# Attention scores taken three head pairs at a time, with one and two steps of context in turn, and 13 row sums a group on TensorE

## What is computed

```python
q = _layernorm_scale_only(q, q_ln_scale)
k = _layernorm_scale_only(k, k_ln_scale)
...
scores = jnp.einsum('bshd,bthd->bhst', q / jnp.sqrt(jnp.float32(HEAD_DIM)), k)
causal = jnp.triu(jnp.ones((S, S), dtype=bool), 1)
scores = jnp.where(causal, NEG_INF, scores)
attn = jax.nn.softmax(scores, axis=-1)
ctx = jnp.einsum('bhst,bthd->bshd', attn, v)
```

## Time and profile before

| | before |
|---|---|
| median of three runs | 2451.99 us (2450.62 to 2453.79) |
| the profiled execution's own time | 2452.69 us |
| its span | 2450.9 us |
| share of the span TensorE is busy | 96% |
| VectorE, ScalarE, GpSimd | 73%, 54%, 11% |
| mean granted TensorE clock | 0.979 |

### The profile page before, as it was taken

The page is one execution under the profiler, slowest core; times in us unless marked ns, Lnnn a source line. Parts: engine busy times, 40 slices in busy tenths (PEclk is TensorE's granted clock), DMA queues, the critical chain, the costliest instruction groups (busy, mean ns, idle before and its releaser), DMA issues. The chain is left out here.

```text
span 2450.9 us, 34384 instructions
## 1 busy us (share of the span) xinstructions
PE 2353.8 (96%) x12546; PEld 1404.8 (57%) x12546; DVE 1787.0 (73%) x1821; ACT 1317.0 (54%) x1631; POOL 266.3 (11%) x266
## 2 busy tenths in 40 slices
PE   8999966999999999999999999959999999999997
PEld 7777742333343333443334433338888888888885
DVE  7666664898988989889898898954555565565654
ACT  4444435888888888888888888811111111111111
POOL 1111111210122001221012110100000000000000
PEclk9999977999999999999999999979999999999999
DMA  7766677010550106401064010072021121110100
GB/s 246 244 222 241 215 217 143 23 32 5 107 115 23 32 5 114 108 23 32 6 117 105 23 32 5 5 265 78 18 69 35 36 64 32 44 50 21 35 18 17
DMA packets 126399, 197.36 MB, mean 81 GB/s; under 512 B 14992, under 2 KB 39568, under 8 KB 126224
## 3 DMA queue, kind: packets, MB, share of 16 engines
q1 hardware_dynamic: 126224, 195.10, 28.5%
HBM read 122.70 MB, written 72.35 MB: 80 GB/s over the span
## 5 line engine op out<-in xcount | busy, mean ns | idle before, releaser
L883 ACT ACTIVATE probs<-score 128x1024 f32<-128x1024 f32 (+3 forms) x1152 | 1025.2, 956 | 212.2 <-PE score L801 188.2
L949 DVE TENSOR_TENSOR total<-total,probs 128x2048 f32<-128x2048 f32 (+3 forms) x472 | 983.2, 2083 | 78.5 <-POOL probs L762 35.7
L801 PE MATMUL score<-qstk,kstk 98*128 98x512 f32 (+3 forms) x2304 | 659.4, 408 | 35.4 <-DMA qstk<-shift 18.6
L801 PEld LDWEIGHTS score<-qstk,kstk 98*128 98x128 f32 x2304 | 378.9, 190 | 527.3 <-ACT probs L883 411.1
L817 PE MATMUL ctx_acc<-probs,values 128*32 128x512 f32 (+3 forms) x4608 | 576.7, 573 | 8.3 <-POOL probs L762 8.3
L1288 ACT ACTIVATE hidden<-slot,gate_scale_sb 128x512 f32<-128x512 f32 x128 | 88.3, 690 | 624.9 <-PE slot L1217 624.9
L762 POOL TENSOR_SCALAR_AFFINE_SELECT probs<-probs 128x512 f32<-128x512 f32 x128 | 188.1, 1470 | 1037.2 <-ACT probs L883 1037.2
L1373 DVE SCALAR_TENSOR_TENSOR hidden<-slot,up_scale_sb,hidden 128x512 f32<-128x512 f32 x128 | 96.0, 750 | 262.4 <-ACT hidden L1288 257.7
L817 PEld LDWEIGHTS ctx_acc<-probs,values 128*32 128x32 f32 x4608 | 92.0, 108 | 202.4 <-issue 163.0
L1217 PE MATMUL slot<-xt_hi,wg_sb 128*128 128x512 f32 x512 | 201.8, 394 | 5.2 <-issue 5.2
L1228 PE MATMUL y<-wd_sb,h_hi 128*128 128x512 f32 x512 | 199.4, 389 | 1.4 <-DVE h_lo L1381 1.4
(11 more groups left out here) (101 smaller groups left out, 1984.4 us busy)
## 6 DMA issues: line engine op xcount, KB each, us to landing
qstk<-q_hi SPq DMA_DIRECT2D x64, 256.0 KB
kstk<-k_hi SPq DMA_DIRECT2D x64, 256.0 KB, 9.4
wq_int<-in_wq SPq DMA_DIRECT2D x48, 256.0 KB, 3.0
wq_float<-wq_f SPq DMA_DIRECT2D x48, 256.0 KB, 2.7
x_raw<-in_x_t SPq DMA_DIRECT2D x32, 256.0 KB, 3.6
v_rows<-v_out SPq DMA_DIRECT2D x32, 256.0 KB, 2.1
q_hi<-part_hi SPq DMA_DIRECT2D x32, 256.0 KB, 2.1
q_lo<-part_lo SPq DMA_DIRECT2D x32, 256.0 KB, 2.5
```

The lines of the kernel that those rows point to most:

```text
L801: ins = pe.matmul(score[u % RING][:, i, cut(t):], kstk[0:ROWS, h, kb * P:(kb + 1) * P], qstk[0:ROWS, q_buffer[ch], h, cut(t):], start=True ...
L883: act.activation(probs[:, t % PB, 2 * p:2 * p + 2, cut(t):], score[u % RING][:, :, cut(t):], ACT.Exp).then_inc(exped, 1)
L949: dve.tensor_tensor(into, into, now, ALU.add).then_inc(added, 1)
```

## The change

`scores` now takes one unit instead of one step. TensorE's order becomes 96 runs a group. Run k takes the scores of the units 3k to 3k + 2 (six matmuls). After an odd k comes the context of the one step 3(k - 1)/2, after an even k the context of the two steps 3k/2 - 2 and 3k/2 - 1. Steps whose number is a multiple of three stand alone, all others in pairs. The rule of `by_pe` becomes: every ninth step of the group, where it is not diagonal and not the first or second of its chunk. That gives the 13 steps 9, 27, 36, 45, 54, 63, 72, 81, 99, 108, 117, 126 and 135. All are multiples of three. Before, the ten were places 10, 20 and 30 of their chunks. The programs of ScalarE, GpSimd, VectorE and SyncE stay, apart from what follows from the new list of sums.

```diff
@@ by_pe
-        return not diagonal(t) and t - first[ch] >= ST * 2 and (t - first[ch]) % 10 == 0
+        return not diagonal(t) and t - first[ch] > 1 and t % 9 == 0
@@ scores
-            def scores(g, t):
+            def scores(g, u):
+
+                t, p = divmod(u, 2)
                 ch, kb = steps[t]
-                if t in first:
+                if p == 0 and t in first:
                     mine = q_chunks[q_buffer[ch]]
                     pe.wait_ge(q_in[q_buffer[ch]], 64 * len(mine) * g + 64 * (mine.index(ch) + 1))
-                if kb == ST * ch:
+                if p == 0 and kb == ST * ch:
                     pe.wait_ge(ones_ready, 1 + ch + 1)
                     pe.wait_ge(k_in[ch], 48 * g + 48)
-                for p in range(2):
-                    u = 2 * t + p
-
-                    pe.wait_ge(exped, 2 * NS * g + u + 1)
-                    for i in range(2):
-                        h = 2 * p + i
...
+                pe.wait_ge(exped, 2 * NS * g + u + 1)
+                for i in range(2):
+                    h = 2 * p + i
...
+            def score_phase(g, k, after):
+
+                for u in range(RING * k, RING * k + RING):
+                    if u < 2 * NS:
+                        scores(g, u)
+                    elif after:
+                        scores(g + 1, u - 2 * NS)
+
+            def weigh_phase(g, k):
+
+                for t in ((3 * k // 2 - 2, 3 * k // 2 - 1) if k % 2 == 0 else (3 * (k // 2),)):
+                    weigh(g, t)
+                    if t - 2 in last:
+                        sum_total(g, last.index(t - 2))
+
             def group(g, after):

-                for t in range(NS):
-                    if t + LAG < NS:
-                        scores(g, t + LAG)
-                    elif after:
-                        scores(g + 1, t + LAG - NS)
-                    weigh(g, t)
-                    if t + LAG - T_LAG in last:
-                        sum_total(g, last.index(t + LAG - T_LAG))
+                for k in range(1, 2 * NS // RING + 1):
+                    score_phase(g, k, after)
+                    weigh_phase(g, k)
                 sum_total(g, NCH - 1)

-            for t in range(LAG):
-                scores(0, t)
+            score_phase(0, 0, False)
```

More of the change, by code:

```diff
@@ L549, in by_pe @@
         ch, kb = steps[t]
-        return not diagonal(t) and t - first[ch] >= ST * 2 and (t - first[ch]) % 10 == 0
+        return not diagonal(t) and t - first[ch] > 1 and t % 9 == 0
     adds = [t for t in range(NS) if not by_pe(t)]
     NA = len(adds)
-    assert NS % PB == 0 and 2 * NS % RING == 0
+    assert NS % PB == 0 and 2 * NS % RING == 0 and NS % 3 == 0
     NM = sum(diagonal(t) for t in range(NS))
@@ L785, in _ @@
             pe.sem_inc(totaled, 2)
-            def scores(g, t):
+            def scores(g, u):
+                t, p = divmod(u, 2)
                 ch, kb = steps[t]
-                if t in first:
+                if p == 0 and t in first:
                     mine = q_chunks[q_buffer[ch]]
                     pe.wait_ge(q_in[q_buffer[ch]], 64 * len(mine) * g + 64 * (mine.index(ch) + 1))
-                if kb == ST * ch:
+                if p == 0 and kb == ST * ch:
                     pe.wait_ge(ones_ready, 1 + ch + 1)
                     pe.wait_ge(k_in[ch], 48 * g + 48)
-                for p in range(2):
-                    u = 2 * t + p
-                    pe.wait_ge(exped, 2 * NS * g + u + 1)
-                    for i in range(2):
-                        h = 2 * p + i
-                        ins = pe.matmul(score[u % RING][:, i, cut(t):], kstk[0:ROWS, h, kb * P:(kb + 1) * P],
-                                        qstk[0:ROWS, q_buffer[ch], h, cut(t):], start=True, stop=True)
-                    ins.then_inc(scored, 1)
+                u = 2 * t + p
+                pe.wait_ge(exped, 2 * NS * g + u + 1)
+                for i in range(2):
+                    h = 2 * p + i
+                    ins = pe.matmul(score[u % RING][:, i, cut(t):], kstk[0:ROWS, h, kb * P:(kb + 1) * P],
+                                    qstk[0:ROWS, q_buffer[ch], h, cut(t):], start=True, stop=True)
+                ins.then_inc(scored, 1)
             def weigh(g, t):
```

## The result

The changed kernel takes 2463.33 us, the median of five runs (2461.84 to 2466.55), beside 2451.99 before: a ratio of 1.0049 (95% interval 1.0034 to 1.0064). It is slower, by 11 us where the prediction has 8, and within its range. The profiled execution has a span of 2463.6 us, 12.7 more than before.

What follows compares the result with a forecast made beforehand. The prediction took TensorE, busy in 96% of the span, as the bound. Waits 18.3 - 2.1, round trips -16.3 and sums +2.6 gave +2.5 us a group, +8.0 in all with the first group's 0.5: 2460 us, range 2446 to 2474.

Steps and rivals of the forecast that it cites:

- Round trips: TensorE's switches between scores and context: 144 become 96, 0.34 us each, -16.3 us a group.
- Sums: Strip matmuls of sums on TensorE: 13 in place of 10, 0.86 us each, +2.6 us a group.
- Ordinary ring waits: Score loads awaiting a buffer after 17 full-width single steps without a sum: 0.26 us each, 4.4 a group.
- Short contexts: After last diagonals of 128 columns (steps 18, 30, 66, 90) the next run comes sooner and waits: 3.6 us a group.
- Evacuations: After chunk ends at steps 3, 39 and 111 the evacuation holds ScalarE and TensorE waits: 3.6 us a group.
- The 11 among diagonals: The other single steps without a sum, standing among diagonals: 0.2 us of wait each, 2.2 a group.
- Masks: TensorE waits for masks of steps 2, 8, 44 and 116: 0.65 us each, 2.6 a group.
- The group's end: TensorE's total sum waits for VectorE's late last add: 1.9 us a group, between 0 and 2.5.
- Before's own waits: Mask waits already in the kernel before, subtracted from the new waits: 2.1 us a group.
- The first group: Early changes hidden behind the wait for a q transfer at its step 12: it keeps +0.5 us.
- no change: Rival: restarted loads cost 0.16 us and masks mostly find VectorE's add over; about 2452 us, chance 0.25.
- Faster: Rival: the ring gives more slack, or masks and last add come in time; 2442 us, down to 2398, chance 0.15.

Runs made afterwards that it cites:

- bare pair: bare_before and bare_order, the old and new orders with half of the exponentials and of VectorE's adds left out: 2437.24 and 2380.16 us.
- sums_only: The kernel before, in its old order, with the thirteen new sums in place of its ten: 2466.68 us, ratio to before 1.0062.
- bare_before: The kernel before with half of each exponential and half of each VectorE add left out: 2437.24 us, ratio 0.9948.
- take_sooner: The changed kernel with VectorE taking a chunk's old sums two steps sooner, ahead of the next chunk's place 3 add: 2454.12 us, ratio to before 1.0013.
- sums_moved: The changed kernel with the sums of steps 27 and 63 moved to steps 33 and 69: 2452.53 us, ratio to before 1.0007.
- bare_order: The new order with the ten old sums and half of each exponential and of each VectorE add left out: 2380.16 us, ratio 0.9712.
- half-exponential pair: half_exp_before and half_exp_order, the old and new orders, both with ten sums and half of each exponential left out: 2440.09 and 2416.86 us.
- half_exp_before: The kernel before with each exponential over one head of its pair instead of two: 2440.09 us, ratio 0.9948.
- ten_single: The new order with ten sums, all on single steps, none at place 3 of a chunk: 2438.59 us, ratio to before 0.9944.
- order_only: The new order with the old ten sums at their old places: 2444.89 us, ratio to before 0.9976.
- seven_late: The new order with seven sums and VectorE taking the old sums two steps sooner: 2443.53 us, ratio to before 0.9961.
- half_exp_order: The new order with the ten old sums and each exponential over one head of its pair: 2416.86 us, ratio 0.9854.

## Why the prediction was right, and where it was off

The time is in the range and the way is the one forecast: slower by 11 us, forecast 8. The terms that the prediction named are all there. But that it came out slower rests on a wait that the prediction didn't name, and in that it was lucky: its own terms, at their measured sizes, sum to nothing. By its steps, for a middle group:

- *Round trips, -16.3.* Right. 0.34 in the timelines, 14.3 us a group in the bare pair.
- *Sums, +2.6.* Right for the matmuls. No run shows the three adds off VectorE alone. In sums_only the group grew by more than the matmuls, so they brought nothing that shows there.
- *Ordinary ring waits, 17 x 0.26 = 4.4.* They are there, 17 of them, at 0.17: 2.9. The restart costs what was said. At step 48 the third exponential ends 3.65 behind the start of the run and not 3.71, and the next run starts at 2.61 and not 2.58, so that 0.09 of the 0.26 went.
- *Short contexts, 3.6.* Measured 3.2. *Evacuations, 3.6.* Measured 3.6 (1.0, 1.0 and 1.5). *The 11 among diagonals, 2.2.* Measured 1.8.
- *Masks, 2.6.* Measured 3.0, 0.67 each and 0.96 at step 2. The middle between the bounds was a choice that came out.
- *The group's end, 1.9.* Measured 1.9.
- *Before's own waits, 2.1.* They are 3.4: the rows show only what the matmul side recorded as idle. bare_before has groups 3.3 to 3.5 us shorter than before's, which says the same.
- **Missed: the sum at place 3** of a chunk that opens the bank, 3.3 us a group. The prediction named `sum_total`'s waits and never asked what a sum in the middle of a chunk waits for. The line stands in `weigh` (`if opens:` with `sums_taken`). Before, the first sum came at place 10, behind VectorE's turn at place 4, and its wait never showed. take_sooner and sums_moved each take back 9 to 11 us with it.
- **Missed: the clock**, 1.7 us where it falls, once in each of the two full middle groups of the profiled execution.
- *The first group, +0.5.* Counted to its step 143 it is 3.3 us shorter than before (687.0 against 690.2). Its end wait (1.9) lies behind that mark, so the forecast is -1.4 up to there. 1.7 of the 3.3 are there by step 11, behind the wait for the q transfer, which is 16.6 us in this trace and 18.6 before. The prediction costs the queues at nothing; sums_only, with the old order, has 21.4, so that this may be scatter. The groups differ by -3.3, +4.8, +4.4 and +3.6, and +3.1 behind the last step 143: together the 12.7 us of the two spans.

The named waits are 1.9 us smaller in sum (16.4 for 18.3) and those of before 1.3 larger, which hid 3.2 of the 5.0 missed. With measured sizes the same sum gives 21.4 - 3.4 - 16.3 + 2.6 = +4.3 us for this group, and the trace has +4.4 (308.9 against 304.5). The step of the prediction that failed is the price of the sums, "3 x 0.86", which took them for matmuls alone: at their new places they cost another 3.3 us a group in waits for the bank.

Without the misses the same sum is 16.4 - 3.4 - 16.3 + 2.6 = -0.7 us a group, no change. take_sooner and sums_moved, which lack the opening and keep nearly all the rest, say the same: 3.1 and 1.5 us above before, under the 4.9 that the prediction can't tell from none, and below the 2457 at which its forecast begins. So on the terms that it weighed, the rival *no change* at 2452 was the right one.

*Faster* assumed that the waits would not come. With none new and the same ten sums its price gives 4 x 16.3 = 65 us. bare_order against bare_before has 57, so the price was about right and the other engines stood against it.

The Trainium skill ("TensorEngine Tiling (Array Packing)", Key Properties) says that a change of tiling mode drains TensorE. The trace agrees in that each round trip costs 0.34 us. The same page, PSUM Bottleneck, says that after a speedup by tiling the copy out of PSUM may bind next. Here TensorE got faster by fewer switches and not by tiling, and the like is seen: the exponentials that empty PSUM take 17 of 23 us in the half-exponential pair.

## What to carry to other kernels

Fewer mode switches are worth their price only as far as the buffers between the engines let the others work on during the longer stretch. Work out one full round: when the consumer's last item ends, and when the producer wants its buffer back. And when work moves to a new place in an engine's order, list every wait on its path, those behind an `if` as well, with the point at which the other engine does its part: the order alone gained 6 us here, thirteen sums for ten in the old order lost 16 of which the matmuls are 10, and the new order with ten sums at better places is 13 us faster than before. Last, ask of a forecast that came true whether its own terms, at their measured sizes, still give it.

## What the runs showed of the hardware

TensorE's granted clock fell from 2.4 to 1.2 GHz for a few us in the middle of the attention. In the changed kernel it did so at 1010 us, after waits of 1.9 us (the group's end), 1.0 (a mask) and 1.5 (an evacuation) within some 14 us, although TensorE's recorded busy share in the stretch ahead of it is 85% (3.38 of 4.00), and at 829, 1.9 us behind the wait of 1.65 at an opening. The second group has the first kind of waits at 700 us and the third has the opening at 1138, and both kept the clock there. In their profiled executions the kernel before, sums_only, half_exp_before, bare_before, ten_single and bare_order keep 1.00 in all middle groups. It fell twice in order_only and take_sooner, three times in seven_late, four times in sums_moved, and for 20 us in all in half_exp_order, which has the longest waits for the last add (4.8). So a few us of waits in one place can cost more than their own length, but not every time, and what decides it wasn't tried.

A mask on GpSimd lasts 0.63 us by itself (1007.12 and 1310.25 in the changed kernel). Where an add of VectorE is under way as it starts, it lasts until 0.5 to 0.6 us after that add's end, in every such mask of both kernels behind 403 us: 2.51 us long in the earlier trace rows.
